# Where the low-rank product of the dense weights is formed: in the last iteration instead of the prologue

## The chip, the cores and the metric

The kernel runs on one core of a Trainium2 chip. The metric is the device time of one execution in microseconds (us), lower is better. All times below are from runs on the chip. One execution before the change was also recorded by the hardware profiler. The engines are called by the profile's names: PE (TensorE), PEld (its weight loads), DVE (VectorE), ACT (ScalarE), POOL (GpSimd) and SP, which here only issues DMAs.

## What is computed

Two residual blocks over `x` of 2 x 512 tokens x 512 features, all in fp32:

```python
x = x + mamba2_mixer(layernorm(x), ...)   # in_proj, conv of 4 taps, 128 heads in 8 groups,
                                          # chunked state-space product, gate, group norm, out_proj
x = x + dense(layernorm(x), W, b, A, B, probs)

def dense(x, W, b, A, B, probs):          # W 512 x 512, 16 experts of rank 16
    out = einsum('bsd,od->bso', x, W) + b
    h = einsum('bsd,erd->bser', x, A)
    return out + einsum('bser,e,eor->bso', h, probs, B)
```

The second block is linear in its normalised input. So the kernel doesn't compute the expert branch for each token: it forms one matrix, `W.T + A.T (probs * B)`, in which the 16 x 16 = 256 rank rows are two blocks of 128 (`ER = 2`), and multiplies by that. This edit is about where that matrix is formed.

## The kernel before

There are two blocks of code, each with a queue of instructions per engine that is written out by hand; engines meet only by semaphores, and at the end of the first block all of them wait for each other.

**Prologue.** It normalises x into `x_high` and `x_low` (an fp32 value split in two parts of fp32r type, so that three fast products give nearly a full fp32 product), projects the first tiles, computes the time steps and stores tables of decays to DRAM, and runs the taps of the first convolutions on DVE. It also forms the dense matrix. SP loads `la`, `lb`, `pr` and `wd` early (L211 to L214). ACT scales `lb` by the probabilities (L425). PE, as the last thing in its queue, runs `lora(k)` for k = 0 to 3: each is `ER` plain fp32 products of 128x512 into one half of `head_bank` (L298), and from k = 2 on waits until an earlier half was copied out. ACT copies each to `dense` (L439), POOL adds `wd` (L271), and SP stores the 1 MB result to `dense_dram` (L249).

**Mixer.** 64 iterations k (8 groups g of 8 units j). In iteration k PE multiplies the out-projection for units before (`out_part`), projects the tiles of the next unit (`project`, L750 to L752), forms `states` (L758), `diagonal` (L769, into `d_bank`) and `carry` (L776). DVE, ACT and POOL convolve, mask, decay, gate and normalise. In the last iteration (k = 63) there is nothing ahead to project. PE's queue in it and behind it is: `later_outs` of unit 62; `states`; `diagonal` of batch 0 and of batch 1 (which wait for `scores` from DVE); `carry` of both batches (which wait for `state` from DVE); two out products; `later_outs` of unit 63; eight `out_part`s; `var_of` (L801), four more out products, and then the tail, in which each of eight token tiles is turned (L820) and multiplied by the dense matrix (`product_of`, L835 to L837).

SP's queue is in order too. In the iteration j = 6 it waits for `y_sum` before the loads of `grown_rows` (L670). Behind them are the bias load (L726) and then the load of the dense matrix (L728):

```python
sp.wait_ge(projected, BATCH * TILES)
sp.dma_start(dense.rearrange("p k d -> p (k d)"), dense_dram).then_inc(dense_in, 16)
```

ACT then copies its four quarters to `dense_high` (L1075), POOL subtracts to `dense_low` (L1409), and `product_of(0)` is the first to need them. The buffers are those of `x_high[:, 0]` and `x_low[:, 0]`, which no projection reads any more.

Of the kernel before, what the change touches and what calls it, by code (L numbers as in the profile page):

```python
# [9 lines left out]
ALU = mybir.AluOpType  # L10
# [79 lines left out]
def build(nc, x, w_in, w_dt, conv_bc, unit_cols, dt_bias, a_log, w_out, w_dense, lora_a, lora_b, probs,  # L90
          bias, out):
    scratch = lambda name, shape: nc.dram_tensor(name, shape, F32, kind="Internal").ap()
    sums_dram = scratch("sums_dram", [BATCH * ALL, PAIR * SEQ])
    grown_dram = scratch("grown_dram", [BATCH * ALL, PAIR * SEQ])

    table_dram = scratch("table_dram", [BATCH, P, 2 * GROUPS, 3 * GH // 2 * CHUNKS])
    chunk_dram = scratch("chunk_dram", [BATCH * GROUPS, GH * CHUNKS])
    dense_dram = scratch("dense_dram", [P, KT * HID])

    x_tokens = x.rearrange("b (c p) d -> p (b c) d", p=P)  # L100
    out_tokens = out.rearrange("b (c p) d -> p (b c) d", p=P)

    with ExitStack() as ctx:
        sb = lambda name, shape, dt=F32: ctx.enter_context(nc.sbuf_tensor(name, shape, dt))
        psum = lambda name, shape: ctx.enter_context(nc.psum_tensor(name, shape, F32))
        banks = (psum("x_bank", [P, BATCH, SEQ]), psum("g_bank", [P, BATCH, SEQ]), psum("d_bank", [P, BATCH, SEQ]),
                 psum("head_bank", [P, BATCH, SEQ]))


        mean_col = sb("mean_col", [P, 2])  # L110
# [12 lines left out]
        loads = ([sem(f"raw_in{i}") for i in range(RAW)], sem("tap_bc_in"), [sem(f"cols_in{i}") for i in range(2)],  # L123
                 [[sem(f"{n}{b}") for b in range(BATCH)] for n in ("sums_stored", "grown_stored", "tables_stored")],
                 sem("dense_stored"), [[sem(f"sums_in{i}_{b}") for b in range(BATCH)] for i in range(2)],
                 [sem(f"grown_in{b}") for b in range(BATCH)])
# [3 lines left out]
        prologue(nc, banks, x_high, x_low, mixed, ident, causal, mean_col, eps_col, buffers, loads, counts, x_tokens,  # L130
                 w_dt, dt_bias, a_log, w_dense, lora_a, lora_b, probs, w_in, conv_bc, unit_cols, dense_dram,
                 sums_dram, grown_dram, table_dram, chunk_dram)
        mixer(nc, banks, x_high, x_low, mixed, ident, causal, mean_col, eps_col, buffers, loads, counts, w_in,
              conv_bc, unit_cols, w_out, bias, dense_dram, sums_dram, grown_dram, table_dram, chunk_dram,
              out_tokens)


def prologue(nc, banks, x_high, x_low, mixed, ident, causal, mean_col, eps_col, buffers, loads, counts, x_tokens, w_dt,
             dt_bias, a_log, w_dense, lora_a, lora_b, probs, w_in, conv_bc, unit_cols, dense_dram, sums_dram,
             grown_dram, table_dram, chunk_dram):  # L140
    raw, w_high, w_low, tap_bc, cols, bc_conv, hs, scores, grown_rows = buffers
    raw_in, tap_bc_in, cols_in, (sums_stored, grown_stored, tables_stored), dense_stored, sums_in, grown_in = loads
# [5 lines left out]
    ER = lora_a.shape[0] // P  # L148
    TURNS = 4
    with ExitStack() as ctx:  # L150
# [6 lines left out]
        dense = sb("dense", [P, KT, HID])  # L157
# [15 lines left out]
        la, lb = sb("la", [P, ER, HID]), sb("lb", [P, ER, HID])  # L173
        pr = sb("pr", [P, ER])
        wd = sb("wd", [P, KT, HID])

        x_in = [sem(f"x_in{tb}") for tb in range(TB)]
        small_in, lora_in, wd_in, mixed_in = sem("small_in"), sem("lora_in"), sem("wd_in"), sem("mixed_in")
# [14 lines left out]
        table_turned, table_ready, lora_ready, lora_product, lora_out, dense_ready = (  # L193
            sem(n) for n in ("table_turned", "table_ready", "lora_ready", "lora_product", "lora_out", "dense_ready"))
# [3 lines left out]
        def _(sp):  # L198
# [49 lines left out]
            sp.wait_ge(dense_ready, KT)  # L248
            sp.dma_start(dense_dram, dense[:].rearrange("p k d -> p (k d)")).then_inc(dense_stored, 16)  # L249
# [3 lines left out]
        def _(pool):  # L253
# [14 lines left out]
            pool.wait_ge(wd_in, 16)  # L268
            for k in range(KT):
                pool.wait_ge(lora_out, k + 1)  # L270
                pool.tensor_tensor(dense[:, k], dense[:, k], wd[:, k], ALU.add).then_inc(dense_ready, 1)  # L271

        @block.tensor
        def _(pe):
# [18 lines left out]

            def lora(k):
                pe.wait_ge(bc_conv_ready, 1)
                reached(pe, lora_out, k - 1)
                for r in range(ER):
                    mm = pe.matmul(head_bank[:, k % 2], la[:, r, k * P:(k + 1) * P], lb[:, r], start=(r == 0),  # L298
                                   stop=(r == ER - 1))
                mm.then_inc(lora_product, 1)  # L300
# [36 lines left out]
            pe.wait_ge(lora_ready, ER)  # L337
            for k in range(KT):
                lora(k)

        @block.scalar
        def _(s):
# [80 lines left out]
            s.wait_ge(lora_in, 48)  # L423
            for r in range(ER):
                s.activation(lb[:, r], lb[:, r], ACT.Copy, scale=pr[:, r:r + 1]).then_inc(lora_ready, 1)  # L425
# [156 lines left out]
def mixer(nc, banks, x_high, x_low, mixed, ident, causal, mean_col, eps_col, buffers, loads, counts, w_in, conv_bc,  # L582
          unit_cols, w_out, bias, dense_dram, sums_dram, grown_dram, table_dram, chunk_dram, out_tokens):
# [4 lines left out]
    raw_in, tap_bc_in, cols_in, (sums_stored, grown_stored, tables_stored), dense_stored, sums_in, grown_in = loads  # L588
# [5 lines left out]
    with ExitStack() as ctx:  # L594
# [35 lines left out]
        dense, dense_high, dense_low = x_high[:, 0].bitcast(F32), x_low[:, 0], x_high[:, 0]  # L630
# [6 lines left out]
        std, rstd = sb("std2", [P, TB]), sb("rstd2", [P, TB])  # L637
        (dense_in, bias_in, mean_ready, ln_std_ready, ln_rstd_ready, xn_ready, xt_turned, xt_high_ready, xt_ready,
# [12 lines left out]
        def _(sp):  # L651
# [39 lines left out]
            def body(g, last):  # L691
                for j in range(UNITS):
# [51 lines left out]
        def _(pe):  # L744
# [94 lines left out]

            def later_outs(j, k):  # L840
# [5 lines left out]
            def body(g, last):  # L846
                for j in range(UNITS):
# [81 lines left out]

            pe.wait_ge(out_low_ready, ALL)  # L930
# [6 lines left out]
            pe.wait_ge(square_added, (UNITS - 1) * GROUPS)  # L937
            var_of()
# [13 lines left out]
        def _(s):  # L952
# [69 lines left out]

            def group_std(done):
# [9 lines left out]
            def body(g, last):  # L1033
                for j in range(UNITS + 1 if last else UNITS):
# [35 lines left out]
                    if j == UNITS:  # L1070
                        group_std(GROUPS)
                    if last and j == UNITS - 1:
                        s.wait_ge(dense_in, 16)
                        for i in range(KT):
                            s.activation(dense_high[:, i], dense[:, i], ACT.Copy).then_inc(dense_high_ready, 1)  # L1075
# [16 lines left out]
            s.wait_ge(dense_stored, 16)  # L1092
# [13 lines left out]
        def _(v):  # L1106
# [109 lines left out]

            def norm_stats(pair):
# [35 lines left out]
            def body(g, last):  # L1253
                for j in range(UNITS):
# [49 lines left out]
            add_outs(GROUPS - 1, UNITS - 1, (2, 3))  # L1304
            add_outs(GROUPS - 1, UNITS, range(CHUNKS))
# [156 lines left out]
```

## Time and profile before

| | |
|---|---|
| median of 3 runs | 1618.51 us |
| the runs | 1618.40, 1618.51, 1619.63 us |
| time of the profiled execution | 1619.32 us |
| its span (first to last instruction) | 1617.6 us |
| mean granted PE clock | 0.998 of full |
| PE busy | 98% of the span |
| DVE, ACT, POOL busy | 77%, 71%, 44% |
| DMA, mean | 102 GB/s |

The profiled execution takes 1.7 us more than its span. Times within the span, such as "at 58.60", are us from its start. Busy shares are means over the whole span; the two places that the edit touches are the 10 us around the end of the prologue and the last 60 us.

### The profile page before, as it was taken

How to read it: one execution, taken by the hardware profiler on the slowest of the kernel's cores; microseconds unless marked ns; L12 is line 12 of the kernel's file. 1: busy time of each engine (PE TensorE's matmuls, PEld its weight loads, DVE VectorE, ACT ScalarE, POOL GpSimd, SP SyncE). 2: the span in 40 equal slices, each digit the busy share in tenths (PEclk: the TensorE clock that was granted, in tenths of full speed). 3: DMA queues.
4: the chain of work that ended last, by engine and by line, in shares of the span. 5: the costliest groups of instructions: out<-in, count | busy, mean ns of one | idle time of the engine just before them, and what ended most of it. 6: DMA issues, size and time to landing. Idle time of an engine off the chain costs nothing. (4 is left out here: it accounts for less than half of the span.)

```text
span 1617.6 us, 26769 instructions
## 1 busy us (share of the span) xinstructions
PE 1589.8 (98%) x9616; PEld 1350.8 (84%) x9616; DVE 1252.3 (77%) x1966; ACT 1156.1 (71%) x2014; POOL 719.4 (44%) x547
## 2 busy tenths in 40 slices
PE   7899999999999999999999999999999999999988
PEld 5678888888888888888888888888888888888876
DVE  6587777877778777787778877787877877777787
ACT  6887667776877677776687766777678767777751
POOL 1264443453534454354453544435444445434543
PEclk9999999999999999999999999999999999999999
DMA  6542422332323233233232232233233323223211
GB/s 202 198 138 86 121 89 83 111 112 73 111 93 111 78 106 101 92 105 95 96 113 91 86 121 89 84 110 111 76 108 102 108 73 116 100 83 111 92 43 52
DMA packets 88244, 164.56 MB, mean 102 GB/s; under 512 B 23344, under 2 KB 39728, under 8 KB 87856
## 3 DMA queue, kind: packets, MB, share of 16 engines
q1 hardware_dynamic: 88112, 162.85, 31.3%
q8 instruction: 77, 1.26, 0.3%
q14 instruction: 55, 0.45, 0.1%
HBM read 157.03 MB, written 5.77 MB: 101 GB/s over the span
## 5 line engine op out<-in xcount | busy, mean ns | idle before, releaser
L1358 POOL TENSOR_TENSOR w_low<-raw,w_high 128x512 fp32r<-128x512 f32 x139 | 179.8, 1293 | 543.6 <-ACT w_high L958 543.6
L1112 DVE SCALAR_TENSOR_TENSOR hs<-x_bank,cols,hs 128x1022 f32<-128x1022 f32 x189 | 241.5, 1278 | 129.6 <-ACT hs L980 127.3
L968 ACT ACTIVATE scores<-scores,tables 128x128 f32<-128x128 f32 x1024 | 312.4, 392 | 1.2 <-DMA tables<-table_dram 1.2
L1372 POOL TENSOR_TENSOR y<-y,gate 128x512 f32<-128x512 f32 x128 | 188.8, 1495 | 205.4 <-DVE y L1174 205.4
L980 ACT ACTIVATE hs<-x_bank,cols 128x1024 f32<-128x1024 f32 x63 | 75.8, 1203 | 278.0 <-PE x_bank L752 278.0
L750 PE MATMUL g_bank<-x_high,w_high 128*128 128x512 f32 x624 | 251.0, 402 | 3.0 <-PEq L150 3.0
L751 PE MATMUL g_bank<-x_low,w_high 128*128 128x512 f32 x624 | 244.0, 391 | 0.0
L752 PE MATMUL g_bank<-x_high,w_low 128*128 128x512 f32 x624 | 243.7, 391 | 0.0
L750 PE MATMUL x_bank<-x_high,w_high 128*128 128x512 f32 x504 | 196.4, 390 | 0.0
L752 PE MATMUL x_bank<-x_high,w_low 128*128 128x512 f32 x504 | 196.1, 389 | 0.0
L751 PE MATMUL x_bank<-x_low,w_high 128*128 128x512 f32 x504 | 196.1, 389 | 0.0
L1137 DVE TENSOR_TENSOR scores<-scores,bc 128x1024 f32<-128x1024 f32 x128 | 169.8, 1332 | 5.4 <-ACT scores L973 5.4
L750 PEld LDWEIGHTS g_bank<-x_high,w_high 128*128 128x128 f32 x624 | 117.4, 188 | 37.1 <-issue 14.5
L1379 POOL TENSOR_TENSOR xdecay<-xdt,tables 128x384 f32<-128x384 f32 x128 | 109.0, 873 | 75.4 <-DVE xdt L1184 75.4
L752 PEld LDWEIGHTS g_bank<-x_high,w_low 128*128 128x128 f32 x624 | 117.6, 188 | 25.4
L973 ACT ACTIVATE scores<-scores 128x1024 f32<-128x1024 f32 x128 | 135.8, 1062 | 2.6
L1366 POOL TENSOR_TENSOR square_sum<-square_sum,gate 128x1024 f32<-128x1024 f32 x56 | 136.1, 2431 | 2.9 <-ACT gate L1021 2.9
L751 PEld LDWEIGHTS g_bank<-x_low,w_high 128*128 128x128 f32 x624 | 117.6, 188 | 22.3
L1151 DVE SCALAR_TENSOR_TENSOR state<-state,chunk_tab,head_bank 128x64 f32<-128x64 f32 x512 | 121.1, 278 | 9.1
L769 PE MATMUL d_bank<-scores,xdt 128*64 128x128 f32 x2048 | 126.2, 276 | 1.5 <-issue 1.5
L1162 DVE TENSOR_TENSOR grown_rows<-head_bank,grown_rows 128x384 f32<-128x384 f32 x128 | 71.3, 557 | 65.6 <-PE head_bank L776 58.4
L769 PEld LDWEIGHTS d_bank<-scores,xdt 128*64 128x64 f32 x2048 | 110.5, 137 | 9.5 <-issue 1.8
(183 smaller groups left out, 3425.8 us busy)
## 6 DMA issues: line engine op xcount, KB each, us to landing
scores<-sums_dram SPq DMA_DIRECT2D x128, 512.0 KB, 4.9
raw<-w_in SPq DMA_DIRECT2D x144, 256.0 KB, 2.9
grown_rows<-grown_dram SPq DMA_DIRECT2D x256, 96.0 KB, 2.8
out_raw<-w_out SPq DMA_DIRECT2D x64, 256.0 KB, 3.4
xt<-x SPq DMA_DIRECT2D x8, 256.0 KB, 5.4
mixed<-x SPq DMA_DIRECT2D x1, 2048.0 KB, 9.3
out<-mixed SPq DMA_DIRECT2D x8, 256.0 KB, 2.0
table_dram<-table SPq DMA_DIRECT2D x2, 768.0 KB, 7.1
```

The source lines that it names most:

```text
L750: pe.matmul(to, w_high[:, slot, k], x_high[:, b, k], start=(k == 0), stop=False)
L751: pe.matmul(to, w_high[:, slot, k], x_low[:, b, k], start=False, stop=False)
L752: mm = pe.matmul(to, w_low[:, slot, k], x_high[:, b, k], start=False, stop=(k == KT - 1))
L769: mm = pe.matmul(d_bank[r * HEAD_DIM:(r + 1) * HEAD_DIM, b, c * P:(c + 1) * P], xdt[:, b, c, r], scores[:, s, b, r, c], start=True, stop=True)
L968: op = s.activation(at, at, ACT.Relu, bias=col[:, r, c:c + 1], scale=-1.0)
L973: s.activation(scores[:, q % 2, b], scores[:, q % 2, b], ACT.Exp, scale=-1.0).then_inc(exp_ready, 1)
L1112: v.scalar_tensor_tensor(out=hs[:, q % 2, :, i:], in0=x_bank[:, :, 0:SEQ - i], scalar=cols[:, q, TAPS - 1 - i:TAPS - i], in1=hs[:, q % 2, ...
L1137: v.tensor_tensor(at, at, bc[:, b].rearrange("p c l -> p (c l)").unsqueeze(1) .to_broadcast([P, PAIR, SEQ]), ALU.mult).then_inc(scores_rea ...
L1151: op = v.scalar_tensor_tensor(out=state[:, b, c, r], in0=state[:, b, c - 1, r], scalar=chunk_tab[:, b, PAIR * q + r, c:c + 1], in1=head_ba ...
L1358: pool.tensor_tensor(w_low[:, slot], raw[:, slot], w_high[:, slot].bitcast(F32), ALU.subtract)\
L1366: pool.tensor_tensor(square_sum[:], square_sum[:], gate[:, q % 2], ALU.add).then_inc(square_added, 1)
L1372: pool.tensor_tensor(y[:, b], y[:, b], gate[:, q % 2, b], ALU.mult).then_inc(y_ready, 1)
```

## The change

Forming the matrix leaves the prologue: its four loads, the scaling of `lb`, the four `lora(k)`, the four copies, the four adds and the store to DRAM. The scratch tensor `dense_dram` is gone. In the last iteration of the mixer:

- SP, behind the bias load, loads `la` (into `bc_conv[:, 1]`), `pr`, `lb` (into `raw`) and `w_dense` (into `scores[:, 0]`).
- ACT scales `lb` in two instructions and then makes `dense_high` of quarters 0 and 1; quarters 2 and 3 follow after the last `finish`.
- PE runs `lora(0)` between `states` and `diagonal`, `lora(1)` between `diagonal` and `carry`, and `lora(2)` and `lora(3)` behind `later_outs` of unit 63, each into one half of `g_bank`.
- DVE adds each product from PSUM to the loaded weights (`dense_of`), which takes the place of a copy on ACT and an add on POOL.
- `var_of` waits for all four quarters.

```diff
 # prologue
-            sp.dma_start(la[:], lora_a.rearrange("(k p) d -> p k d", p=P)).then_inc(lora_in, 16)
-            sp.dma_start(lb[:], lora_b.rearrange("(k p) d -> p k d", p=P)).then_inc(lora_in, 16)
-            sp.dma_start(pr[:], probs).then_inc(lora_in, 16)
-            sp.dma_start(wd[:], w_dense.rearrange("(k p) d -> p k d", p=P)).then_inc(wd_in, 16)
...
-            sp.wait_ge(dense_ready, KT)
-            sp.dma_start(dense_dram, dense[:].rearrange("p k d -> p (k d)")).then_inc(dense_stored, 16)
...
-            pool.wait_ge(wd_in, 16)
-            for k in range(KT):
-                pool.wait_ge(lora_out, k + 1)
-                pool.tensor_tensor(dense[:, k], dense[:, k], wd[:, k], ALU.add).then_inc(dense_ready, 1)
...
-            pe.wait_ge(lora_ready, ER)
-            for k in range(KT):
-                lora(k)
...
-            s.wait_ge(lora_in, 48)
-            for r in range(ER):
-                s.activation(lb[:, r], lb[:, r], ACT.Copy, scale=pr[:, r:r + 1]).then_inc(lora_ready, 1)
...
-            for k in range(KT):
-                s.wait_ge(lora_product, k + 1)
-                s.activation(dense[:, k], head_bank[:, k % 2], ACT.Copy).then_inc(lora_out, 1)
 # mixer
+        la, lb = bc_conv[:, 1], raw[:, 0:ER].rearrange("p r k f -> p r (k f)")
+        dense = scores[:, 0].rearrange("p b r c l -> p (b r) (c l)")
...
                         sp.dma_start(bias_row, bias.partition_broadcast(P)).then_inc(bias_in, 16)
-                        sp.wait_ge(projected, BATCH * TILES)
-                        sp.dma_start(dense.rearrange("p k d -> p (k d)"), dense_dram).then_inc(dense_in, 16)
+                        sp.wait_ge(c_ready, GROUPS)
+                        sp.dma_start(la, lora_a.rearrange("(k p) d -> p k d", p=P)).then_inc(la_in, 16)
+                        sp.dma_start(pr[:], probs).then_inc(lb_in, 16)
+                        sp.wait_ge(w_low_ready, TILES)
+                        sp.dma_start(lb, lora_b.rearrange("(k p) d -> p k d", p=P)).then_inc(lb_in, 16)
+                        sp.wait_ge(diag_done, BATCH * (ALL - 1))
+                        sp.dma_start(dense, w_dense.rearrange("(k p) d -> p k d", p=P)).then_inc(dense_in, 16)
...
+            def lora(k):
+                pe.wait_ge(lb_ready, ER)
+                pe.wait_ge(la_in, 16)
+                reached(pe, dense_ready, k - 1)
+                for r in range(ER):
+                    mm = pe.matmul(g_bank[:, k % 2], la[:, r, k * P:(k + 1) * P], lb[:, r], start=(r == 0),
+                                   stop=(r == ER - 1))
+                mm.then_inc(lora_product, 1)
...
                     for b in range(BATCH):
                         states(k, b)
+                    if not ahead:
+                        pe.wait_ge(gate_ready, BATCH * ALL)
+                        lora(0)
                     for b in range(BATCH):
                         reached(pe, added, emptied(k - 1, 2 + b))
                         diagonal(k, s, b)
+                    if not ahead:
+                        lora(1)
...
             later_outs(UNITS - 1, ALL - 1)
+            lora(2)
+            lora(3)
...
             pe.wait_ge(square_added, (UNITS - 1) * GROUPS)
+            pe.wait_ge(dense_ready, KT)
             var_of()
...
+                        s.wait_ge(lb_in, 32)
+                        for r in range(ER):
+                            s.activation(lb[:, r], lb[:, r], ACT.Copy, scale=pr[:, r:r + 1]).then_inc(lb_ready, 1)
+                        for i in range(2):
+                            dense_part(i)
...
+            def dense_of(k):
+                v.wait_ge(dense_in, 16)
+                v.wait_ge(lora_product, k + 1)
+                v.tensor_tensor(dense[:, k], g_bank[:, k % 2], dense[:, k], ALU.add).then_inc(dense_ready, 1)
...
+                    if last and j == UNITS - 1:
+                        dense_of(0)
                     skip(j, k)
+                    if last and j == UNITS - 1:
+                        dense_of(1)
...
             y_low_part(UNITS - 1, ALL - 1)
             add_outs(GROUPS - 1, UNITS - 1, (2, 3))
+            dense_of(2)
+            dense_of(3)
```

## Rows read from the trace of the kernel before

**Rows 1.** The page, part 1: busy time, share of the span, instructions.
```profile
PE 1589.8 (98%) x9616; PEld 1350.8 (84%) x9616; DVE 1252.3 (77%) x1966; ACT 1156.1 (71%) x2014; POOL 719.4 (44%) x547
```

**Rows 2.** Timeline of PE around the end of the prologue: start, duration, count, [idle before].
```profile
48.62 7.03 PE L298 MATMUL head_bank<-lb,la 128*128 128x512 f32 x16
58.60 0.47 PE L750 MATMUL g_bank<-x_high,w_high 128*128 128x512 f32 x1 [2.95 <-PEq L150]
```

**Rows 3.** Timelines of DVE, SP and ACT around the same stretch.
```profile
50.91 3.91 DVE L533 SCALAR_TENSOR_TENSOR hs<-x_bank,cols,hs 128x1022 f32<-128x1022 f32 x3
47.48 2.79 SPq L236 DMA_DIRECT2D table_dram<-table  x2
52.03 2.73 SPq L246 DMA_DIRECT2D grown_rows<-grown_dram  x4
57.65 0.33 SPq L249 DMA_DIRECT2D dense_dram<-dense  x1
34.92 1.33 ACT L425 ACTIVATE lb<-lb,pr 128x512 f32<-128x512 f32 x2
64.36 2.45 ACT L968 ACTIVATE scores<-scores,tables 128x128 f32<-128x128 f32 x8 [1.19 <-DMA tables<-table_dram]
```

**Rows 4.** Busy time by stretch: its length, then PE, PEld, DVE, ACT, POOL, granted clock, DMA share, GB/s.
```profile
55.70:58.60 2.90, 0.00 (x0) 0.03 (x1) 0.00 (x0) 0.77 (x2) 1.46 (x2) 1.00 0.88 313
59.40:62.80 3.40, 3.40 (x10) 2.63 (x9) 0.00 (x0) 3.39 (x5) 0.00 (x0) 0.50 0.84 329
```

**Rows 5.** DMA issues of the first 70 us: count, KB each, median us from issue to landing.
```profile
la<-lora_a SPq DMA_DIRECT2D x1, 512.0 KB, 4.9
lb<-lora_b SPq DMA_DIRECT2D x1, 512.0 KB, 5.4
wd<-w_dense SPq DMA_DIRECT2D x1, 1024.0 KB, 8.1
table_dram<-table SPq DMA_DIRECT2D x2, 768.0 KB, 7.1
tables<-table_dram SPq DMA_DIRECT2D x2, 48.0 KB, 5.3
```

**Rows 6.** Timeline of PE in the last iteration and up to `var_of`.
```profile
1557.78 1.09 PE L769 MATMUL d_bank<-scores,xdt 128*64 128x128 f32 x16
1560.41 1.09 PE L769 MATMUL d_bank<-scores,xdt 128*64 128x128 f32 x16 [1.54 <-issue]
1563.79 0.94 PE L776 MATMUL head_bank<-c_feat,state 128*128 128x128 f32 x6 [2.28 <-DVE state L1151]
1565.01 1.65 PE L776 MATMUL head_bank<-c_feat,state 128*128 128x128 f32 x6 [0.28 <-DVE state L1151]
1578.16 1.84 PE L801 MATMUL g_bank<-mean_col,square_sum 128*128 128x2 f32 x16
```

**Rows 7.** Timelines of SP, DVE and POOL there.
```profile
1551.24 2.36 SPq L670 DMA_DIRECT2D grown_rows<-grown_dram  x4
1554.28 0.43 SPq L728 DMA_DIRECT2D x_high<-dense_dram  x1
1563.97 0.98 DVE L1151 SCALAR_TENSOR_TENSOR state<-state,chunk_tab,head_bank 128x64 f32<-128x64 f32 x4
1568.81 0.69 DVE L1204 TENSOR_TENSOR acc<-x_bank,acc 128x512 f32<-128x512 f32 x1 [0.62 <-PE x_bank L809]
1575.33 4.99 POOL L1409 TENSOR_TENSOR x_high<-x_high,x_low 128x512 fp32r<-128x512 f32 x4
```

**Rows 8.** DMA issues between 1545 and 1565, columns as in the fifth group.
```profile
x_high<-dense_dram SPq DMA_DIRECT2D x1, 1024.0 KB, 7.4
grown_rows<-grown_dram SPq DMA_DIRECT2D x4, 96.0 KB, 2.7
```

**Rows 9.** Busy time by stretch in the last iteration, columns as in the fourth group.
```profile
1565.00:1566.00 1.00, 0.99 (x4) 1.00 (x5) 1.00 (x1) 0.00 (x0) 0.00 (x0) 0.50 0.00 0
```

More of the change, by code:

```diff
@@ L124, in build @@
                  [[sem(f"{n}{b}") for b in range(BATCH)] for n in ("sums_stored", "grown_stored", "tables_stored")],
-                 sem("dense_stored"), [[sem(f"sums_in{i}_{b}") for b in range(BATCH)] for i in range(2)],
+                 [[sem(f"sums_in{i}_{b}") for b in range(BATCH)] for i in range(2)],
                  [sem(f"grown_in{b}") for b in range(BATCH)])
@@ L130, in build @@
         prologue(nc, banks, x_high, x_low, mixed, ident, causal, mean_col, eps_col, buffers, loads, counts, x_tokens,
-                 w_dt, dt_bias, a_log, w_dense, lora_a, lora_b, probs, w_in, conv_bc, unit_cols, dense_dram,
+                 w_dt, dt_bias, a_log, w_in, conv_bc, unit_cols,
                  sums_dram, grown_dram, table_dram, chunk_dram)
         mixer(nc, banks, x_high, x_low, mixed, ident, causal, mean_col, eps_col, buffers, loads, counts, w_in,
-              conv_bc, unit_cols, w_out, bias, dense_dram, sums_dram, grown_dram, table_dram, chunk_dram,
-              out_tokens)
+              conv_bc, unit_cols, w_out, w_dense, lora_a, lora_b, probs, bias, sums_dram, grown_dram, table_dram,
+              chunk_dram, out_tokens)
 def prologue(nc, banks, x_high, x_low, mixed, ident, causal, mean_col, eps_col, buffers, loads, counts, x_tokens, w_dt,
-             dt_bias, a_log, w_dense, lora_a, lora_b, probs, w_in, conv_bc, unit_cols, dense_dram, sums_dram,
-             grown_dram, table_dram, chunk_dram):
+             dt_bias, a_log, w_in, conv_bc, unit_cols, sums_dram, grown_dram, table_dram, chunk_dram):
     raw, w_high, w_low, tap_bc, cols, bc_conv, hs, scores, grown_rows = buffers
-    raw_in, tap_bc_in, cols_in, (sums_stored, grown_stored, tables_stored), dense_stored, sums_in, grown_in = loads
+    raw_in, tap_bc_in, cols_in, (sums_stored, grown_stored, tables_stored), sums_in, grown_in = loads
     (w_high_ready, w_low_ready, projected, bc_tap0_ready, bc_tap_chain, bc_conv_ready, tap0_ready, tap_chain,
@@ L156, in prologue @@
         table = sb("table", [P, BATCH, 2 * GROUPS, 3, GH // 2 * CHUNKS])
-        dense = sb("dense", [P, KT, HID])
         chunk_decay = sb("chunk_decay", [P, BATCH, CHUNKS])
@@ L192, in prologue @@
                              "grown_ready", "chunk_ready", "decay_ready"))
-        table_turned, table_ready, lora_ready, lora_product, lora_out, dense_ready = (
-            sem(n) for n in ("table_turned", "table_ready", "lora_ready", "lora_product", "lora_out", "dense_ready"))
+        table_turned, table_ready = sem("table_turned"), sem("table_ready")
         block = ctx.enter_context(nc.Block())
@@ L292, in dt_of @@
                 mm.then_inc(dt_product, 1)
-            def lora(k):
-                pe.wait_ge(bc_conv_ready, 1)
-                reached(pe, lora_out, k - 1)
-                for r in range(ER):
-                    mm = pe.matmul(head_bank[:, k % 2], la[:, r, k * P:(k + 1) * P], lb[:, r], start=(r == 0),
-                                   stop=(r == ER - 1))
-                mm.then_inc(lora_product, 1)
             def project(t, b):
@@ L582, in mixer @@
 def mixer(nc, banks, x_high, x_low, mixed, ident, causal, mean_col, eps_col, buffers, loads, counts, w_in, conv_bc,
-          unit_cols, w_out, bias, dense_dram, sums_dram, grown_dram, table_dram, chunk_dram, out_tokens):
+          unit_cols, w_out, w_dense, lora_a, lora_b, probs, bias, sums_dram, grown_dram, table_dram, chunk_dram,
+          out_tokens):
     x_bank, g_bank, d_bank, heads = banks
@@ L587, in mixer @@
     raw, w_high, w_low, tap_bc, cols, bc_conv, hs, scores, grown_rows = buffers
-    raw_in, tap_bc_in, cols_in, (sums_stored, grown_stored, tables_stored), dense_stored, sums_in, grown_in = loads
+    raw_in, tap_bc_in, cols_in, (sums_stored, grown_stored, tables_stored), sums_in, grown_in = loads
     (w_high_ready, w_low_ready, projected, bc_tap0_ready, bc_tap_chain, bc_conv_ready, tap0_ready, tap_chain,
@@ L628, in mixer @@
                              "std_ready", "rstd_ready", "out_done", "added", "mixed_ready"))
-        dense, dense_high, dense_low = x_high[:, 0].bitcast(F32), x_low[:, 0], x_high[:, 0]
+        ER = lora_a.shape[0] // P
+        la, lb = bc_conv[:, 1], raw[:, 0:ER].rearrange("p r k f -> p r (k f)")
+        dense = scores[:, 0].rearrange("p b r c l -> p (b r) (c l)")
+        dense_high, dense_low = x_low[:, 0], x_high[:, 0]
+        pr = sb("pr", [P, ER])
         bias_row = bc_conv[:, 0, 0]
@@ L637, in mixer @@
         std, rstd = sb("std2", [P, TB]), sb("rstd2", [P, TB])
+        la_in, lb_in, lb_ready, lora_product, dense_ready = (
+            sem(n) for n in ("la_in", "lb_in", "lb_ready", "lora_product", "dense_ready"))
         (dense_in, bias_in, mean_ready, ln_std_ready, ln_rstd_ready, xn_ready, xt_turned, xt_high_ready, xt_ready,
@@ L1021, in finish, with dense_part @@
                     s.activation(gate[:, q % 2], y[:], ACT.Square).then_inc(squared, 1)
+            def dense_part(i):
+                s.wait_ge(dense_ready, i + 1)
+                s.activation(dense_high[:, i], dense[:, i], ACT.Copy).then_inc(dense_high_ready, 1)
             def group_std(done):
@@ L1070, in body @@
                     if j == UNITS:
+                        for i in range(2, KT):
+                            dense_part(i)
                         group_std(GROUPS)
                     if last and j == UNITS - 1:
-                        s.wait_ge(dense_in, 16)
-                        for i in range(KT):
-                            s.activation(dense_high[:, i], dense[:, i], ACT.Copy).then_inc(dense_high_ready, 1)
+                        s.wait_ge(lb_in, 32)
+                        for r in range(ER):
+                            s.activation(lb[:, r], lb[:, r], ACT.Copy, scale=pr[:, r:r + 1]).then_inc(lb_ready, 1)
+                        for i in range(2):
+                            dense_part(i)
             silu_bc(0, 0)
```

9 lines of the change are left out of this document (1 added, 8 removed).

## Prediction

> **What bounds the kernel now.** I read the page first: PE is busy 98% of the span [rows 1], so over the 64 iterations only what PE does or waits for counts, and the other engines have room. What PE doesn't do is at the ends, so I read PE's timeline there, and for each gap the timeline of the engine that ends it. Around the end of the prologue the reader should see that PE's last work is the 16 records of `lora`, from 48.62 to 55.65, and that PE then idles 2.95 us until the mixer starts at 58.60 [rows 2]. In the last iteration PE waits three times, 1.54, 2.28 and 0.28 us [rows 6]: for `scores` and `state` from DVE. Behind it PE runs without a gap to `var_of` at 1578.16. What follows `var_of` (the group's deviation, the normalisation, the turns, the products) hangs on it on all engines, so a delay of `var_of` delays the end by the same.
>
> **Removed: the start gains 2.8 us.** The last things in the prologue are in this order: fourth `lora`, ACT's copy, POOL's add, SP's store, which is issued at 57.65 and takes 0.33 to issue; PE's first mixer instruction comes 0.62 us behind that [rows 2, 3]. With this chain gone, the next to end are DVE's taps, 50.91 + 3.91 = 54.82, and SP's issues of `grown_rows`, 52.03 + 2.73 = 54.76 [rows 3]. Neither has anything to do with the edit. So PE starts at 54.82 + 0.62 = 55.44, which is 3.16 us earlier. The scaling on ACT (1.33 us, [rows 3]) is worth nothing: the DVE chain, not ACT, ends the prologue. The four loads, 2 MB, are issued behind all that the prologue first needs; nothing either.
>
> Two things take from the 3.16. First the clock. In the kernel before, PE idles 2.9 us and the granted clock then is 0.50, the 1.2 GHz level, from 59.40 to 62.80 [rows 4]; the first 0.8 us of the mixer were still at full clock. Without `lora` PE idles from 48.7 to 55.4, so I expect half clock from the mixer's first instruction; up to 0.8 us more at half clock costs up to 0.4, and I take 0.3. Second the DMAs. ACT waits 1.19 us for the `tables` until 64.36 [rows 3], and the queues are 0.88 full before the mixer starts [rows 4]. The two table stores are issued at 47.48 and 50.0 and land 7.1 us later, at 54.6 and 57.1 [rows 3, 5], so SP's first load can be issued at about 55.3, and the second, behind its store, at 57.2; at 5.3 us each they land at 60.6 and 62.5 [rows 5]. The 1 MB store that is queued ahead of them today is gone, which helps them. So ACT moves by about what PE moves. Bounds: 3.2 if neither costs anything; 0.5 if the queue is so full that the tables come hardly earlier. I take 2.8, near the first, because the store that goes is the largest single transfer between.
>
> **Added: `var_of` comes 7.1 us later.** The steps on PE's path, from the end of `states` at 1557.78 to `var_of`:
>
> - Today it takes 1578.16 - 1557.78 = 20.4 us. In it are 4.1 us of waits [rows 6], and one stretch at half clock [rows 9]; the like stretch in the prologue was 3.4 us long [rows 4], so it costs half of that, 1.7. What is left is 14.6 us of work at full clock.
> - `lora` adds its own 16 records. They took 7.03 us at full clock [rows 2]. Nothing in the move makes them shorter. The adds on DVE take 0.69 each, as `acc` does [rows 7], and are needed two products later: hidden.
> - `lora(0)` stands ahead of both diagonals in PE's queue and waits for the scaled `lb`. SP can't reach these loads before the `grown_rows` loads are released at 1551.24 and issued, and then the bias; the first load behind these is issued at 1554.28 [rows 7]. That will be `la`; `lb` follows behind it and `pr`, at about 1555.2 by 0.45 us for an issue. When does `lb` land? The row nearest is the dense load: 1 MB issued at 1554.28 landed 7.4 us later, at 1561.7 [rows 8]. `la` and `lb` are together the same 1 MB, at the same place in the queue, so I take 1561.5. Scaling takes ACT 1.33 [rows 3], so PE can begin at 1562.8, a wait of 5.0 us. Behind `lora(0)` are queued both diagonals, `lora(1)`, the carries; DVE's `skip` and, behind it, `carry_part`, and so POOL and ACT, wait for these. DVE's `state` is ready by 1564.95 [rows 7], before the carries are reached, so that wait of today disappears into this one.
> - The clock: PE idles 5 us, more than the 2.9 that brought half clock in the prologue [rows 4]. I expect the one stretch at 0.50 earlier than today, from about 1561.4, with its first part falling in the idle time: cost 0.9.
>
> Sum: 14.6 + 7.0 + 5.0 + 0.9 = 27.5 against 20.4, which is 7.1 us later. `dense_high` and `dense_low` no longer have long slack, but POOL's four subtractions take 4.99 us [rows 7] and can start with the `squared` part, near 1579, so they end near 1584.5, before `product_of(0)` at about 1595. The `w_dense` load is last in the queue: 8.1 us by the row of `wd` [rows 5] from 1555.7, so 1563.8, still before `lora(0)` ends at 1565.5. Hidden.
>
> Bounds for the landing of `lb`: not before 1555.2 + 2.7 = 1557.9, the landing time of the small `grown_rows` loads here [rows 8]; 1560.6 by its own 5.4 us in the prologue, where the queues were fuller [rows 5]; not after 1555.2 + 7.4 = 1562.6 [rows 8]. With these `var_of` comes 2.4, 6.4 and 7.9 us later (for the first, see the rival).
>
> The Trainium skill ("DMA: Bandwidth & Descriptors", section on the anatomy of one DMA) fits a DMA's time as about 2.0 us plus its bytes at 436 GB/s. For 1 MB that is 4.4 us, and the row of the dense load has 7.4 us, so this trace doesn't bear it out for a queue with other loads ahead. By that rule of the Trainium skill both operands would be there at 1558.7, the wait for `lb` would be 2.2 us, and the sum would be some 3 us smaller.
>
> **Total.** -2.8 + 7.1 = +4.3 us. The sum is made in the profiled execution (span 1617.6, its own time 1619.32). The median of the runs is 1618.51, 0.8 below that; the difference is put on the median: 1622.8 us. A measurement here can tell about 0.2%, 3.2 us, from no change, so this is slower by a little more than that.
>
> **Rivals.**
>
> - *The operands come early, and `lora` fills PE's waits.* If `lb` lands by 1558, `lora(0)` begins at 1559.3 and ends at 1561.1, the diagonals (1.9 us) at 1563.0, `lora(1)` at 1564.7, the carries at 1566.2; PE never idles long, so the slow stretch goes too; then 10.9 us of out products and 3.5 of `lora(2)` and `(3)`: `var_of` at 1580.6, +2.4, and in total -0.4: 1618.1, no change. For it: little else is in the queue, 96 KB loads take 2.7 us [rows 8]. Against it: the 1 MB load at the same place took 7.4. It decides below a landing of about 1559.9, where the total passes +3.2. By the rule of the Trainium skill quoted above the time would be about 1619.7, which lies in this case too. Chance of the whole case, up to +3.2: 0.30.
> - *The forecast*, total +3.3 to +5.5: 0.50.
> - *The start gives little.* The early tables or the longer slow stretch take most of the 3.16; with 0.5 left the total is +6.6, 1625.1. For it: the full queues [rows 4]. Against it: the missing store. Or, at the end, a second stretch at half clock, 1.7 us more: +6.0, 1624.5. Chance 0.16.
> - *Faster.* The start gains 3.2 and the tail gives back nothing: `lora(2)` and `(3)` would have to lie beside something, and PE has no gap there [rows 6]; that would be 1615. Chance 0.04.
>
> **Range.** 1618.0 to 1625.2: from the early operands to the start that gives little. The forecast alone has 1621.5 to 1624.5. Faster by over 0.2%: 0.04. Within 0.2%: 0.32. Slower: 0.64.
>
> **What would show it.** In the changed profile: first `project` of the mixer at 55.4, half clock from its first record, `scores` on ACT near 61.5; everything in the iterations 2.8 us earlier. In the last iteration a wait of some 5 us on PE ahead of `lora(0)`, ended by ACT's `lb`, and ACT itself waiting for a DMA; both diagonals together behind it; no wait for `state`; `var_of` 27.5 us behind the end of `states`. The prediction is wrong if `lb` lands before 1560 in the old count, if the mixer doesn't start some 3 us earlier, or if the tail behind `var_of` waits for `dense_low`.

## The result

| | before | after |
|---|---|---|
| median of 7 runs | 1618.40 us | 1624.54 us |
| the runs | 1617.83 to 1620.00 | 1623.43 to 1626.49 |
| profiled execution: its time, its span | 1619.32, 1617.6 | 1624.54, 1622.8 |
| mean granted PE clock | 0.998 | 0.996 |

The ratio is 1.0034, with a 95% interval of 1.0024 to 1.0044: 5.5 us slower, between 3.9 and 7.1; the two medians of the table lie 6.1 us apart, inside that interval. The forecast was 4.3 us slower. In the profiles the span grew by 5.2 us. Two points of PE's timeline split it. `states` of iteration 63 begins 2.7 us earlier than before, and from there to `var_of` it takes 8.0 us longer (29.80 instead of 21.81). Behind `var_of` both kernels take the same: 39.4 us to the end of the span.

The start, timelines of PE, SP and ACT of the kernel after:

```profile
48.14 0.63 PE L294 MATMUL d_bank<-ident,decay 128*128 128x128 f32 x4 [0.36 <-ACT table L376]
55.68 0.77 PE L727 MATMUL g_bank<-x_high,w_high 128*128 128x512 f32 x1 [6.91 <-PEq L147]
62.97 0.82 PE L772 MATMUL head_bank<-ident,bc_conv 128*128 128x128 f32 x6
...
55.49 0.33 SPq L650 DMA_DIRECT2D tables<-table_dram  x1
...
61.49 2.45 ACT L962 ACTIVATE scores<-scores,tables 128x128 f32<-128x128 f32 x8 [1.24 <-DMA tables<-table_dram]
```

The first `project` of the mixer is at 55.68, 2.92 us earlier than the 58.60 of [rows 2], with 6.91 us of idle PE ahead of it. ACT gets to `scores` at 61.49, 2.87 earlier than in [rows 3], and waits for the tables as long as before (1.24, before 1.19).

The last iteration, timeline of PE of the kernel after, which answers to [rows 6]:

```profile
1553.64 1.50 PE L735 MATMUL head_bank<-xdecay,b_tok 128*128 128x128 f32 x12
1559.77 3.75 PE L822 MATMUL g_bank<-raw,bc_conv 128*128 128x512 f32 x4 [4.62 <-ACT raw L1075]
1563.45 2.53 PE L746 MATMUL d_bank<-scores,xdt 128*64 128x128 f32 x32
1565.91 1.98 PE L822 MATMUL g_bank<-raw,bc_conv 128*128 128x512 f32 x4
1567.73 1.50 PE L753 MATMUL head_bank<-c_feat,state 128*128 128x128 f32 x12
...
1574.55 3.59 PE L822 MATMUL g_bank<-raw,bc_conv 128*128 128x512 f32 x8
...
1583.44 1.84 PE L778 MATMUL g_bank<-mean_col,square_sum 128*128 128x2 f32 x16
```

Three things are to be seen. PE waits 4.62 us for the scaled `lb` (L1075), and all else in the iteration stands behind that wait. The four records of `lora(0)` take 3.75 us, those of `lora(1)` 1.98: the same work at half clock and at full. And the waits for `state` are gone; both `carry` run as one row.

The releaser of that wait, timelines of SP and ACT and the DMA issues between 1545 and 1570:

```profile
1552.91 0.43 SPq L703 DMA_DIRECT2D raw<-lora_b  x1
...
1558.33 1.33 ACT L1075 ACTIVATE raw<-raw,pr 128x512 f32<-128x512 f32 x2 [3.80 <-DMA raw<-lora_b]
...
scores<-w_dense SPq DMA_DIRECT2D x1, 1024.0 KB, 7.5
bc_conv<-lora_a SPq DMA_DIRECT2D x1, 512.0 KB, 5.0
raw<-lora_b SPq DMA_DIRECT2D x1, 512.0 KB, 5.4
```

Busy time by stretch (length, PE, PEld, DVE, ACT, POOL, granted clock, DMA share, GB/s), which answers to [rows 9]:

```profile
1557.80:1557.90 0.10, 0.00 (x0) 0.00 (x0) 0.10 (x1) 0.00 (x0) 0.10 (x1) 0.56 0.89 348
...
1559.77:1564.60 4.83, 4.83 (x16) 2.29 (x18) 3.02 (x12) 0.25 (x1) 0.00 (x0) 0.50 0.05 20
...
1564.60:1564.70 0.10, 0.10 (x4) 0.10 (x2) 0.00 (x0) 0.10 (x1) 0.00 (x0) 0.80 0.00 0
```

The clock falls at 1557.8, when PE has been idle for 2.7 us, and comes back at 1564.6: 6.8 us at the 1.2 GHz level, in 4.8 of which PE is busy. Half of that busy time, 2.4 us, is what the slow clock costs. In the kernel before the granted clock is 0.50 from 1564.7 to 1568.1, with PE busy in 3.1 us of it: 1.6 us.

### The profile page after: what moved, and what is told of

Its sections match the earlier page's. It is cut to its first block and busy times, and to the rows that moved or that the text cites. A ratio compares the mean times of both kernels' runs of the same rounds, so it can differ in the third digit from the quotient of the medians.

```text
span 1622.8 us, 26767 instructions
## 1 busy us (share of the span) xinstructions
PE 1590.5 (98%) x9616; PEld 1350.7 (83%) x9616; DVE 1256.0 (77%) x1970; ACT 1154.4 (71%) x2010; POOL 714.3 (44%) x543
```

## The experiments

In the table, "states 63" is the start of `states` in iteration 63 in the profile, "stretch" the time from there to the start of `var_of`. What stands ahead of the first belongs to the start and to the iterations, what lies in the second to the end, and behind it all take the same (39.3 to 39.5 us). Span, "states 63" and stretch are those of one profile, the ratio is that of all runs.

| kernel | states 63 | stretch | span | ratio to before, 95% interval |
|---|---|---|---|---|
| before | 1556.35 | 21.81 | 1617.6 | 1 |
| after | 1553.64 | 29.80 | 1622.8 | 1.0034 (1.0024 to 1.0044) |
| after_again | 1553.57 | 30.99 | 1623.9 | 1.0034 (1.0021 to 1.0046) |
| no_lora | 1552.73 | 21.66 | 1613.8 | 0.9983 (0.9974 to 0.9993) |
| late_lora | 1554.00 | 29.19 | 1622.6 | 1.0032 (1.0019 to 1.0045) |
| warm_wait | 1554.44 | 28.50 | 1622.3 | 1.0022 (1.0012 to 1.0031) |
| early_loads | 1553.66 | 23.81 | 1616.8 | 0.9994 (0.9985 to 1.0004) |
| early_scale | 1552.48 | 23.78 | 1615.7 | 0.9997 (0.9987 to 1.0006) |
| warm_start | 1552.64 | 30.38 | 1622.4 | 1.0036 (1.0024 to 1.0049) |
| before_warm | 1555.19 | 22.21 | 1616.8 | 0.9997 (0.9988 to 1.0006) |
| late_ylow2 | 1552.56 | 22.60 | 1614.5 | 0.9986 (0.9977 to 0.9995) |
| late_ylow2_again | 1553.55 | 22.61 | 1615.5 | 0.9990 (0.9981 to 0.9999) |
| before_ylow | 1555.79 | 22.14 | 1617.4 | 0.9993 (0.9984 to 1.0001) |
| best2 | 1553.85 | 22.60 | 1615.8 | 0.9986 (0.9977 to 0.9994) |

### The start alone: no_lora

The prologue as after, and nothing put into the last iteration:

```diff
                     for b in range(BATCH):
                         states(k, b)
-                    if not ahead:
-                        pe.wait_ge(gate_ready, BATCH * ALL)
-                        lora(0)
...
-            lora(2)
-            lora(3)
```

> The kernel after without any low-rank product: no loads of its operands, no lora on PE, no adds; the loaded w_dense is used as the matrix (the low-rank term is left out of the result). This is the removal from the prologue alone. Theory 1 (the start gives what the drained chain gave, the end takes more): span 1614.9, that is 2.7 us below the kernel before, all of it won before the first iteration. Rival (the start only looks shorter and gives the time back in the iterations, because ACT and the table loads bind there): span 1616.5 or more.

The span is 1613.8, 3.8 below before, and the ratio 0.9983, which is 2.7 us. What the start gives is kept through the 64 iterations: `states` of iteration 63 is 3.6 us earlier, and the stretch is that of before (21.66). The first theory holds. The size moves by profile: in the nine profiles with this same prologue and nothing else changed ahead of that point (after, after_again, no_lora, late_lora, warm_wait, early_loads, early_scale and both of late_ylow2), `states` of iteration 63 begins between 1552.48 and 1554.44, on average at 1553.40; in the two with the old prologue (before, before_ylow) at 1556.35 and 1555.79. The difference of the averages is 2.7.

### The work without the wait: late_lora

```diff
-            lora(2)
-            lora(3)
+            for k in range(KT):
+                lora(k)
...
-            dense_of(2)
-            dense_of(3)
+            for k in range(KT):
+                dense_of(k)
```

(the calls of `lora` and `dense_of` inside iteration 63 are gone; ACT makes all four `dense_high` behind the last `finish`.)

> The kernel after with all four lora behind later_outs of unit 63, so that PE never waits for the scaled lb; the waits for scores and state from DVE come back. Theory 1 (PE's 7.0 us of extra products are the main cost, and the wait for lb only replaces waits of before): the end costs 7.0 instead of 8.0, span 1621.8. Rival (the wait for lb, with its slow clock, is the cost; the products fit in when nothing waits): span 1618 or less.

```profile
1558.08 1.09 PE L746 MATMUL d_bank<-scores,xdt 128*64 128x128 f32 x16 [1.55 <-issue]
1561.45 2.93 PE L753 MATMUL head_bank<-c_feat,state 128*128 128x128 f32 x12 [2.28 <-DVE state L1145]
1570.87 7.03 PE L822 MATMUL g_bank<-raw,bc_conv 128*128 128x512 f32 x16
1577.33 0.79 PE L784 MATMUL x_bank<-out_high,y_high 128*128 128x512 f32 x1
```

```profile
1560.00:1566.70 6.70, 5.25 (x18) 4.71 (x19) 5.62 (x16) 0.17 (x1) 1.18 (x1) 0.50 0.07 28
```

These are its timeline of PE and its busy time in the stretch at half clock, with the columns of [rows 4]. The 16 records take 7.03 us, to the digit what they took in the prologue [rows 2], and PE's old waits for `scores` and `state` are back (1.55, 2.28). On PE's path they cost a little less than their row is long: the next product starts 6.46 us after the first of them, since the end of the row overlaps with it. The stretch is 29.19: 7.4 above before, 0.6 below after. The other 0.9 us is mostly the clock. It is at half for 6.8 us here, though PE's waits in this iteration are those of before, where it is at half for 3.4. The rival, that the wait for `lb` is the cost and nothing else, falls: without that wait the kernel is as slow (1.0032). Equally, what `lora(0)` and `(1)` take when they stand in the middle isn't hidden in after: the wait of 4.6 us and 2.4 us of slow clock are more than the 4.1 us of waits and 1.6 us of slow clock whose place they take. Added up, 6.7 us for the products (from row start to row start in the timeline of late_ylow2, below, where nothing waits), 4.6 and 2.4, less 4.1 and 1.6, give 8.0, which is what the stretch grew by.

### The clock during the wait: warm_wait

```diff
                         pe.wait_ge(gate_ready, BATCH * ALL)
+                        for _ in range(20):
+                            pe.matmul(g_bank[:, 0], w_high[:, 0, 0], x_high[:, 1, 0], start=True, stop=True)
                         lora(0)
```

> The kernel after with 20 fp32r products of 128x512 ahead of lora(0), whose results lora(0) overwrites: they fill the 4.6 us wait for the scaled lb. If half clock during lora(0) and the diagonals costs what its stretch says, 4.9 us busy at half clock, the span falls by about 2.4, to 1620.4. If the slowness of these records has another cause (their operands or the loads arriving), nothing changes: 1622.8.

```profile
1555.69 4.79 PE L857 MATMUL g_bank<-x_high,w_high 128*128 128x512 f32 x20
1561.62 1.98 PE L822 MATMUL g_bank<-raw,bc_conv 128*128 128x512 f32 x4 [1.13 <-ACT raw L1077]
1563.53 1.97 PE L746 MATMUL d_bank<-scores,xdt 128*64 128x128 f32 x32
1565.43 1.98 PE L822 MATMUL g_bank<-raw,bc_conv 128*128 128x512 f32 x4
```

From the start of `lora(0)` to that of `lora(1)` it takes 3.81 us instead of 6.14: 2.3 us given back, as expected, and `lora(0)` takes 1.98. The span fell by only 0.5, because it held two other things: in this profile `lora(0)` starts 7.18 us behind the start of `states`, since `lb` was ready later, where in after it is 6.13; and iteration 63 began 0.8 later. So the cost of the clock is shown on its own stretch, and the span of this profile alone would have hidden it. By runs the ratio is 1.0022 beside 1.0034, and the intervals of the two overlap. The profiled execution, at 1624.05, was also the longest of the nine; their median is 1623.40, and four of them lie between 1620.86 and 1621.72, a little below the 1622.1 that the expected span comes to as a time.

### Operands one iteration earlier: early_loads and early_scale

```diff
+                    if last and j == UNITS - 2:
+                        sp.wait_ge(c_ready, GROUPS)
+                        sp.dma_start(la, ...)   # and pr, lb, moved from j == UNITS - 1
                     if ahead:
                         for b in range(BATCH):
                             load_grown(ahead[2], b)
```

> The kernel after with the loads of la, pr and lb one iteration earlier, ahead of the waiting grown_rows loads; the scaling stays where it is on ACT. lb is then there when ACT comes to it, PE's wait for it falls from 4.6 to about 0.8 us, and there is too little idle time for the clock to fall before the diagonals. Theory 1: the own waits for scores and state come back in part; span about 1618.5 (4.3 less than after), still above before less the start's 2.7. If work on PE were the only cost and waits didn't matter: 1622.8 as after.

Timelines of SP, ACT and PE of early_loads:

```profile
1530.53 1.05 SPq L698 DMA_DIRECT2D raw<-lora_b  x1
1548.55 2.76 SPq L642 DMA_DIRECT2D grown_rows<-grown_dram  x4
...
1554.45 1.32 ACT L1076 ACTIVATE raw<-raw,pr 128x512 f32<-128x512 f32 x2
...
1555.87 1.96 PE L823 MATMUL g_bank<-raw,bc_conv 128*128 128x512 f32 x4 [0.71 <-issue]
1557.76 1.97 PE L747 MATMUL d_bank<-scores,xdt 128*64 128x128 f32 x32
```

`lb` is issued 22 us earlier, since SP no longer has to be through the last `grown_rows` first. PE's wait is 0.71 instead of 4.62, the clock stays at full, and the stretch falls from 29.80 to 23.81. The kernel is as fast as before (0.9994). This is the rival of the prediction in which the operands come early: it was priced at +2.4 for the stretch and is +2.0. The 6.0 us that come off the stretch are about the 3.9 of wait and the 2.4 of clock. The expected 1618.5 was 1.7 too careful, for it let the old waits come back. Moving the scaling too:

```diff
                         decays(k + 1, ahead[1], 0)
+                        if last and j == UNITS - 2:
+                            s.wait_ge(lb_in, 32)
+                            for r in range(ER):
+                                s.activation(lb[:, r], lb[:, r], ACT.Copy, scale=pr[:, r:r + 1]).then_inc(lb_ready, 1)
                         silu_hs(k + 1, (j + 1) % 2)
```

> As the kernel with the early loads, and ACT scales lb already in iteration 62, in a wait of 1.56 us that it has there. lora(0) can then follow states at once (0.7 us of wait on PE gone). Theory 1 with DVE's state as the next thing that ends last: PE arrives earlier at the carries but waits there for state, so the span falls by at most 0.3, 1616.5. If PE's own work alone set the end, it falls by 0.7, 1616.1.

The stretch is 23.78, the same: PE comes 0.7 earlier and waits 0.38 and 0.28 us for DVE's `state`, which has become what ends last. By runs it is also no faster (0.9997 beside 0.9994). (The span of 1615.7 is lower because this profile's start was.)

### DVE's order: late_ylow2, and the same on the kernel before

```diff
-                    if prev:
+                    if prev and not (last and j == UNITS - 1):
                         y_low_part(prev[1], prev[2])
...
                     for b in range(BATCH):
                         carried_state(*now, b)
+                    if last and j == UNITS - 1:
+                        y_low_part(prev[1], prev[2])
```

(and a wait for that `y_low_part` ahead of the last `skip`, which writes the `y` that `y_low_part` reads.)

> As early_scale, and in iteration 63 DVE makes state before the y_low part of unit 62 (2.28 us) instead of behind it. From states of iteration 63 to var_of it took 23.78 us in early_scale, with 0.66 us of waits for state on PE. If state on DVE sets the end of the carries, these waits go and the stretch is 23.1 us; the y_low part and skip then come later on DVE, and if they now end last (out products of unit 63 or y_high), the stretch is as long or longer than 23.8.

> late_ylow2 once more, beside the kernel before with the same order on DVE. If the move with early operands is worth something by itself, it is 0.5 us or more below before_ylow by the span from the first project to the end and by the median; if the order is all, they are equal.

> The kernel before, with the prologue's low-rank product as it was, and only the order of DVE in iteration 63 changed: state before the y_low part of unit 62. Here PE waits 2.28 and 0.28 us for state. If these waits go and nothing else comes to end last, the span falls by 2.3 to 1615.3, and the gain of late_ylow2 over before comes from this order and not from the move; if DVE's later y_low and skip end last instead, it falls by less than 1.

The stretch falls to 22.60 and again 22.61, and the kernel is faster than before: 0.9986 and 0.9990, both intervals below 1. On the kernel before, the same order does not shorten the stretch in the profiled execution (22.14, before 21.81), though PE's wait for `state` went from 2.28 and 0.28 to 0.28. PE's timeline of before_ylow shows what is late next, and late_ylow2's shows what stands in the same place there:

```profile
1562.25 0.94 PE L776 MATMUL head_bank<-c_feat,state 128*128 128x128 f32 x6 [0.28 <-DVE state L1151]
...
1572.14 0.80 PE L807 MATMUL d_bank<-out_high,y_high 128*128 128x512 f32 x1 [2.10 <-DVE acc L1204]
1572.73 0.63 PE L808 MATMUL d_bank<-out_low,y_high 128*128 128x512 f32 x1
```

```profile
1566.28 3.59 PE L823 MATMUL g_bank<-raw,bc_conv 128*128 128x512 f32 x8
1575.16 1.84 PE L779 MATMUL g_bank<-mean_col,square_sum 128*128 128x2 f32 x16
```

In before_ylow PE arrives early at the out products behind unit 63 and waits 2.10 us for `acc` on DVE, which stands behind the last `y_low_part`, which waits for ACT's `y_high` and POOL's gate; then it runs 0.63 us a record at half clock. In the moved kernels `lora(2)` and `lora(3)` stand between `later_outs` and those products, just where that wait would be. In late_ylow2 PE has no wait left from `states` to `var_of`, and the clock stays at full; the added products then make the stretch only 0.8 us longer than in before (22.60 and 21.81). They stand in the place of 4.1 us of waits and of the slow clock. So most of the added work does find cover, once everything ahead of it is early enough, but not all of it: the gain of late_ylow2 over before is still the start's.

Whether the move is worth more than the order alone is not shown. The expectation asked for 0.5 us or more between late_ylow2_again and before_ylow. The medians are 1617.48 and 1617.26, and from the first `project` to the end the moved kernel takes longer (1559.8 and 1558.5 us). The spans of the two profiles, 1615.5 and 1617.4, say otherwise only by the execution that was caught: before_ylow's eleven runs fall into two groups, six from 1616.08 to 1617.26 and five from 1618.53 to 1619.65, and the profiled one (1619.13) is of the second. The first group is where the expected fall of 2.3 us would put it. No profile of a run of that group exists, so what differs between the groups stays open; the wait for `acc` and the slow clock behind it are shown for the second only.

### The clock at the start: warm_start, before_warm, best2

```diff
             for i in range(1, 6):
                 turn_table(i)
+            pe.wait_ge(bc_conv_ready, 1)
+            for _ in range(26):
+                pe.matmul(head_bank[:, 0], w_high[:, 2, 0], x_high[:, 1, 0], start=True, stop=True)
```

> The kernel after with 26 fp32r products of 128x512 behind the last table turn of the prologue, in the time in which PE idles 6.9 us; their results are overwritten. They keep the clock at 2.4 GHz. The first 24 products of the mixer then take 5.5 instead of 7.3 us. If PE alone set the first iteration the span falls by 1.8 to 1621.0; but ACT's chain from the table loads (scores) reaches PE with only about 0.8 us to spare, so I expect 0.8, 1622.0, with a new wait of PE for scores or xdecay in the first iteration.

> The kernel before with 9 overwritten fp32r products of 128x512 behind its last lora, in the 2.95 us in which PE idles. If the half clock of the first iteration comes from this idle time, it goes, the first 24 products take 5.5 instead of 7.2 us, and PE reaches the first states 1.6 us earlier; ACT's scores have only some 0.7 us to spare, so the span falls by 0.7, to 1616.9. If the clock would fall anyway, 1617.6.

> late_ylow2 and the 26 overwritten products at the end of the prologue together. The first alone gave -0.1 to -0.7 us on early_scale by the theory, the second 1.0 us up to iteration 63 in the kernel after. If they are independent, span 1614.4, some 3 us below the kernel before; by the median then about 0.998 of it.

Timeline of PE of warm_start:

```profile
55.53 0.47 PE L730 MATMUL g_bank<-x_high,w_high 128*128 128x512 f32 x1 [0.84 <-PEq L147]
69.90 1.50 PE L738 MATMUL head_bank<-xdecay,b_tok 128*128 128x128 f32 x12
72.39 2.23 PE L749 MATMUL d_bank<-scores,xdt 128*64 128x128 f32 x32 [0.99 <-issue]
```

The first `states` comes 14.37 us after the first `project` instead of 16.1, so half clock at the mixer's start did come from the idle time and costs 1.7 us on PE. But PE then waits 0.99 us ahead of the first `diagonal`, for `scores`: ACT itself waits 2.03 us for the tables there, where it waited 1.24 in after. `states` 63 comes 1.0 us earlier than in after, which is less than the nine profiles above differ among themselves, and by runs nothing is won (1.0036 beside 1.0034); the span is 1622.4 where 1622.0 was expected. before_warm does the same in the kernel before: a wait of 0.80 us in the same place, `states` 63 at 1555.19, 1.16 earlier than in before and 0.6 earlier than in before_ylow, and a span 0.8 below before, as expected; by runs (0.9997) it can't be told from before. In best2 the waiting is 1.35 us, it began the mixer 1.0 us later than late_ylow2, and by runs the two are equal (0.9986): the warm start adds nothing that can be measured to late_ylow2. The expected sum of 1614.4 was not reached.

### How far one profile can be trusted: after_again

> The kernel after once more, for how far a second profile of one program agrees with the first: the first project of the mixer at 55.7 give or take 0.6, and states of iteration 63 to var_of at 29.8 give or take 0.6, by where in the tail the clock falls.

The first `project` is at 56.06 and `states` 63 at 1553.57, within the stated 0.6. The stretch is 30.99, 1.2 longer, twice the bound: PE's wait is 5.65 us instead of 4.62. SP issues `lb` 0.6 us later (1553.52), because its four `grown_rows` issues take 3.40 us instead of 2.72, and it lands 5.7 us after that instead of 5.4. The medians agree (1624.54 and 1623.99). So one profile gives the wait for `lb` to about 1 us only.

## Why the prediction was right, and where it was off

- **Slower, by the start's gain less the end's loss: right.** Forecast +4.3 us, measured +5.5 (3.9 to 7.1) by runs and +5.2 by the spans. The case called the forecast reached from +3.3 to +5.5, so the result lies at its upper edge. What took it there is what the prediction named in its third case, a second stretch at half clock at the end, with 1624.5 as the time; the median is 1624.54. It had given that case, together with a start that gives little, 0.16, and the agreement to the digit is luck, since the other terms moved too.
- **The start: right, 2.8 against 2.7.** The mixer was put at 55.44 and is at 55.68. Half clock from the first record was right. The 24 products from the mixer's first to `turn_b` take 7.29 us instead of 7.16, which is 0.1 where 0.3 was taken; over the nine profiles with the new prologue they take 7.19 to 7.95, on average 7.46, which is 0.3. ACT's `scores` were put near 61.5 and are at 61.49. The bound of 0.5 for tables that come no earlier was never approached.
- **The work of `lora`: right.** The records take 7.03 us against 7.03 in late_lora. As a term on PE's path this is 0.4 to 0.6 too much, because the row's end overlaps with the next product (6.46 us from start to start there).
- **The wait for `lb`: 5.0 forecast, 4.62 and 5.65 in two profiles.** The landing time was the weak term: it was taken from the 1 MB load in the same place as 6.3 us after the issue and was 5.4, which is what `lb` took in the prologue [rows 5]. The rule of the Trainium skill ("DMA: Bandwidth & Descriptors", anatomy of one DMA) that was weighed is a fit for DMAs that POOL issues. It gives 3.2 us for 512 KB and 4.4 for `la` and `lb` together, against the 5.0 and 5.4 measured for these, which SP issues; the trace stays above it with other loads ahead in the queue. The prediction's two other landings, with `var_of` 6.4 and 7.9 us later, come out of its own terms as 6.2 and 8.2 if only the wait changes; nothing hangs on them.
- **The clock at the end: mis-sized.** The step said "I expect the one stretch at 0.50 earlier than today, from about 1561.4, with its first part falling in the idle time: cost 0.9". The clock was at half for 6.8 us, twice the length of the one stretch of [rows 4], with PE busy in 4.8 of it: 2.4 us lost. warm_wait gave back 2.3 of it. This term, 1.5 us too small, with a wait 0.4 too large, takes the forecast of 27.5 us from the end of `states` to `var_of` to 28.6; 28.4 were measured, and the overlap named above can hold the rest. The step that the prediction took from [rows 4], that one wait brings one stretch of 3.4 us, does not hold as a rule: with the same waits of 1.5 and 2.3 us on PE in the last iteration it was 3.4 us in before and no_lora and 6.8 in late_lora and before_warm.
- **What was costed at nothing: right.** `w_dense` landed at 1553.39 + 7.5 = 1560.9, before `lora(0)` ended; the tail waits for neither `dense_low` nor the four quarters.
- **The rival with the early operands** was right in its mechanism and nearly in its price, and wrong in its condition for this kernel: SP reaches the loads too late. early_loads supplies the condition and gets about that time (a ratio of 0.9994; the rival had 1618.1).

## What to carry to other kernels

Here, work moved from a drained chain into a saturated queue cost its full time on that queue (late_lora, +7.4 us) unless it stood where the queue waited, and it only stood there when its operands were early (early_loads, +2.0): count the issue of each load behind whatever its queue waits for first. Put the wait for new operands nowhere ahead of work that is already late; the wait for `lb` cost its length and then, on PE, 2.4 us by the clock of what followed. And when a wait is taken away, look for what is late next before counting it: here `state`, then `acc`, and at the start ACT's `scores`. And ask of a profile where its execution lies among the runs: before_ylow's and warm_wait's lay in the slower part.

## What the runs showed that was not expected

DVE's second `scores` and `y_low_part` take about twice as long in the last two iterations as in the one before them, in before as in after, while POOL works beside them. Timelines of DVE and POOL of the kernel after, and then the same `y_low_part` in late_ylow2, where POOL's work ended at 1557.65:

```profile
1553.09 1.22 DVE L1138 TENSOR_TENSOR scores<-scores,bc 128x1024 f32<-128x1024 f32 x1
1554.84 2.77 DVE L1138 TENSOR_TENSOR scores<-scores,bc 128x1024 f32<-128x1024 f32 x1
1557.53 2.28 DVE L1129 SCALAR_TENSOR_TENSOR y_low<-y,cols,y_high 128x1024 fp32r<-128x1024 f32 x1
...
1553.60 2.92 POOL L1378 TENSOR_TENSOR square_sum<-square_sum,gate 128x1024 f32<-128x1024 f32 x1 [0.37 <-ACT gate L1015]
1556.48 2.24 POOL L1407 TENSOR_TENSOR out_low<-out_raw,out_high 128x512 fp32r<-128x512 f32 x1
```

```profile
1558.87 1.28 DVE L1131 SCALAR_TENSOR_TENSOR y_low<-y,cols,y_high 128x1024 fp32r<-128x1024 f32 x1
```

`out_low` itself takes 2.24 us, and 2.28 in the iteration before; in the 62 iterations ahead of those it takes about 1.3, and so does `y_low_part`. The ends in the timeline read as if the two engines took turns: the second `scores` ends 1.1 us after `square_sum`, `out_low` 1.1 us after `scores`, `y_low_part` 1.1 us after `out_low`, a little less than each takes elsewhere (1.2 to 1.3). The Trainium skill ("GPSIMD Engine Reference", Specifications) says that POOL's access to SBUF is shared with DVE and contends with DVE's instructions of two SBUF inputs; these have two, and the 2.28 against 1.28 agrees. No run takes POOL's instruction away, so the cause is argued and not shown. Of the 1.2 us that late_ylow2 won in the stretch over early_scale, 0.66 are the two waits for `state`, which are gone; that the rest is the end of this overlap is not shown. Open too is what decides how long the clock stays at half: 3.4 us around the start of the mixer in before and 6.8 in after, and 3.4 or 6.8 us in the last iteration with the same waits.
